# A mask write on VectorE for one score block in eight, with the value wave moved between two scores

## The reference

```
energy = einsum('nqhd,nkhd->nhqk', q, k)             # 16 heads of 32, 512 queries, 8192 keys
energy = where(mask == 0, -1e20, energy)
attention = softmax(energy / sqrt(512), axis=3)
out = einsum('nhql,nlhd->nqhd', attention, v) @ Wo.T + bo
x = x + out
```

## Time and profile before

| what | us |
|---|---|
| median of three runs | 4054.88 |
| the profiled execution, its own time | 4055.3 |
| its span, first to last instruction | 4053.6 |
| loop of the first attention in it, heads 0 to 14 up to the last maxima | 939.3 (417.85 to 1357.15) |
| a head of that loop, from one start to the next | 62.8 |

### The profile page before, as it was taken

The page is one execution under the profiler, slowest core; times in us unless marked ns, Lnnn a source line. Parts: engine busy times, 40 slices in busy tenths (PEclk is TensorE's granted clock), DMA queues, the critical chain, the costliest instruction groups (busy, mean ns, idle before and its releaser), DMA issues. The chain is left out here.

```text
span 4053.6 us, 51692 instructions
## 1 busy us (share of the span) xinstructions
PE 3772.0 (93%) x17986; PEld 2220.6 (55%) x17986; DVE 2806.8 (69%) x3519; ACT 2340.7 (58%) x3659; POOL 1873.0 (46%) x1133
## 2 busy tenths in 40 slices
PE   9999999999999976789999899999999988869998
PEld 7887444444444342247888644444444435448886
DVE  4334877777777368945888877777777644668888
ACT  2224677777777735423777626666666641537775
POOL 1001687787877718920000147888888830000001
PEclk9999999999999987889999979999999999979999
DMA  9997566666666512022888767777777640328887
GB/s 355 327 339 247 136 155 153 159 152 156 152 156 152 127 60 83 0 97 85 323 317 322 285 176 173 172 168 174 176 175 172 133 113 32 84 90 323 322 320 264
DMA packets 298957, 750.50 MB, mean 185 GB/s; under 512 B 56878, under 2 KB 90414, under 8 KB 264906
## 3 DMA queue, kind: packets, MB, share of 16 engines
q1 hardware_dynamic: 249306, 569.44, 41.7%
q0 software_dynamic: 49392, 177.76, 21.9%
HBM read 475.44 MB, written 98.96 MB: 142 GB/s over the span
## 5 line engine op out<-in xcount | busy, mean ns | idle before, releaser
L1026 ACT ACTIVATE prob<-psum 128x512 f32<-128x512 f32 x1628 | 918.0, 598 | 402.4 <-PE psum L902 373.1
L1222 POOL TENSOR_TENSOR den_pool<-den_pool,prob 128x1024 f32<-128x1024 f32 x405 | 1018.7, 2515 | 87.4 <-DVE den_pool L1127 33.2
L902 PE MATMUL psum<-q_stack,k_ring 98*128 98x512 f32 x2048 | 961.3, 500 | 20.5 <-ACT prob L1026 16.8
L1098 DVE CUSTOM_DVE_ANT_0 psum<-psum,mask_q 128x1024 f32<-128x1024 f32 x512 | 627.0, 1234 | 229.2 <-PE psum L864 213.4
L1094 DVE TENSOR_REDUCE row_max<-psum 128x1 f32<-128x1024 f32 x512 | 609.9, 1219 | 225.1 <-PE psum L864 219.5
L902 PEld LDWEIGHTS psum<-q_stack,k_ring 98*128 98x128 f32 x2048 | 395.7, 194 | 526.0 <-ACT psum L1032 199.2
L864 PE MATMUL psum<-k_ring,q_stack 96*128 96x512 f32 x2048 | 670.2, 409 | 12.0 <-DMA q_stack<-prob 5.2
L1982 DVE TENSOR_TENSOR weight_lo<-weight_raw,weight_hi 128x2048 fp32r<-128x2048 f32 x180 | 411.1, 2290 | 113.8 <-ACT weight_hi L1978 113.5
L913 PE MATMUL psum<-prob,x 128*32 128x512 f32 x3256 | 474.7, 608 | 3.2 <-ACT prob L1026 0.8
L864 PEld LDWEIGHTS psum<-k_ring,q_stack 96*128 96x128 f32 x2048 | 389.7, 194 | 97.8 <-issue 18.0
L2157 POOL DMA_DIRECT2D y_slots<-xnT x28 | 15.3, 548 | 860.0 <-ACT xnT L2261 860.0
(11 more groups left out here) (468 smaller groups left out, 6582.7 us busy)
## 6 DMA issues: line engine op xcount, KB each, us to landing
den_dma<-prob POOLq DMA_DIRECT2D x211, 512.0 KB, 5.1
k_ring<-k_hi SPq DMA_DIRECT2D x1024, 64.0 KB, 2.3
weight_raw<-in_L_ffn_Wu SPq DMA_DIRECT2D x60, 1024.0 KB, 7.3
weight_raw<-in_L_ffn_Wd SPq DMA_DIRECT2D x60, 1024.0 KB, 5.5
weight_raw<-in_L_ffn_w SPq DMA_DIRECT2D x60, 1024.0 KB, 6.6
den_dma<-xnT POOLq DMA_DIRECT2D x72, 512.0 KB, 5.0
k_ring<-k_lo SPq DMA_DIRECT2D x512, 64.0 KB, 2.6
w_o<-in_L_ffn_w SPq DMA_DIRECT2D x30, 1024.0 KB, 7.3
```

Source lines behind the costliest of these rows:

```text
L902: e.matmul(out, k_ring[:, n % kring, kt * P:(kt + 1) * P], q_stack[h % n_q][:], start=not masked, stop=True, skip_group_check=masked and b ...
L1026: e.activation(prob[b // 2 % n_p][:, b % 2, :], bank_of("block", b), ACT.Exp, scale=scale).then_inc(s_exp, 1)
L1098: e.tensor_tensor_reduce(out=max_banks(q), in0=max_banks(q), in1=masks[0][:, i, 2 * c2 * KC:2 * (c2 + 1) * KC], scale=1.0, scalar=-3.0e38, ...
L1222: e.tensor_tensor(den[:], den[:], tile, ALU.add).then_inc(s_dpool, 1)
```

## The change

Every block with b % 8 == 1, the second block of each step with g % 4 == 0, gets its mask from VectorE instead of from TensorE. VectorE's `mask_first` waits until the bank is free, writes `mask_k` times 2^67 into it with one `tensor_scalar`, and raises `s_predve`. It stands in VectorE's queue ahead of the reduction of the same step. On TensorE the mask matmul of that block is gone, its score waits for `s_predve` and adds to what lies in the bank, and in those steps the wave comes ahead of score 2g+1 instead of behind it. The sixteen heads have 128 such blocks.

```
+    def act_masks(b):
+        return masked and b % 4 == 2
+    def dve_masks(b):
+        return masked and b % 8 == 1
...  scores(b), TensorE
-                if masked and b % 4 == 2:
+                mask_is_there = act_masks(b) or dve_masks(b)
+                if act_masks(b):
                     e.wait_ge(s_pre, b // 4 + 1)
+                elif dve_masks(b):
+                    e.wait_ge(s_predve, b // 8 + 1)
                 else:
                     wait_for_bank(e, "block", b)
-                if masked and b % 4 != 2:
+                if masked and not mask_is_there:
                     e.matmul(out, k.ident_big[:], masks[1][:, t, :], start=True, stop=False)
                 e.matmul(out, k_ring[:, n % kring, kt * P:(kt + 1) * P], q_stack[h % n_q][:],
-                         start=not masked, stop=True, skip_group_check=masked and b % 4 == 2).then_inc(s_score, 1)
+                         start=not masked, stop=True, skip_group_check=mask_is_there).then_inc(s_score, 1)
...  the loop over steps, TensorE
+                if dve_masks(2 * g + 1):
+                    waves_after(h, p)
                 scores(2 * g + 1)
                 for q in second:
                     maxima(q)
-                waves_after(h, p)
+                if not dve_masks(2 * g + 1):
+                    waves_after(h, p)
...  VectorE
+            def mask_first(b):
+                wait_for_bank(e, "block", b)
+                e.tensor_scalar(bank_of("block", b), masks[1][:, b % KT, :], BIG, None, ALU.mult).then_inc(s_predve, 1)
...  the loop over steps, VectorE
+                if dve_masks(2 * g + 1):
+                    mask_first(2 * g + 1)
                 for q in maxima_at(g):
                     if q < H * PAIRS:
                         maxima(q)
```

More of the change, by code:

```diff
@@ L749, in cross_attention @@
     s_score, s_exp, s_wave = k.sem("s_score"), k.sem("s_exp"), k.sem("s_wave")
-    s_pre = k.sem("s_mask_first")
+    s_pre, s_predve = k.sem("s_mask_first"), k.sem("s_mask_first_dve")
     s_ddve, s_dpool, s_dsum = k.sem("s_den_dve"), k.sem("s_den_pool"), k.sem("s_den_sum")
```

## The result

The changed kernel takes 4064.43 us, the median of 18 runs (4059.87 to 4073.66), against 4056.56 for the kernel before (18 runs). The ratio of the two is 1.0022, 95% interval 1.0015 to 1.0028: slower by two parts in a thousand, within the bound of 0.3% that the prediction set for "no change". The profiled execution has a span of 4058.7, 5.1 more than before.

A forecast was written before the change was run, and what follows sets the result against it. The loop was taken to run at TensorE's pace. Fifteen heads +5.2, three heads more +1.2, head 0 +0.8 and head 15 +0.8 summed to +8.0 us on 4055.3, so 4063; range 4048 to 4080.

The forecast's parts named there:

- The ordinary step: Masked step away from VectorE's adds: the wave covers VectorE's mask, and TensorE saves one matmul, 0.22 us.
- The mask's length: VectorE's mask instruction: 0.69 us, taken from the 128x512 copy with one operand in PSUM.
- Steps 4 and 8: Where VectorE's adds put it behind: TensorE waits for late masks, 1.17 us in step 8; a head 1.47 late at step 9.
- Step 28: Late in each head, where `top_of_rows` holds VectorE: the mask is seen after TensorE wants it, 0.2 us lost.
- heads 4, 8 and 12: Heads with reciprocals: VectorE another 0.3 us behind in step 28 and 0.1 in step 24; +1.2 us for the three.
- step 24: In the three heads with reciprocals: these put VectorE 0.1 us behind there.
- Head 0: Its step 0 has no wave and saves nothing (+0.2); the mask meets a full VectorE chain at loop start, +0.8 us.
- Head 15: No maxima before the wave, which moves ahead by only 0.15 to 0.2; 0.1 us lost a step, +0.8 in all.
- what fifteen heads have in common: Per head +1.47 from steps 4 and 8, -1.32 from six other steps, +0.20 from step 28: +0.35, in all +5.2 us.
- cover everywhere: Rival: masks of steps 4 and 8 come in time, 119 or so save 0.22 each, -26 us, 4029; chance 0.10 with unseen gains.

The follow-up runs named there:

- e1: Changed kernel, with the masks of steps 4 and 8 of each head back on TensorE and the wave behind the scores there; ratio 0.9976 to the kernel before.
- e2: Kernel before with the wave moved as in the changed kernel, but every mask of VectorE left out and written by TensorE; ratio 0.9978 to the kernel before.
- e6: Changed kernel, with VectorE's adds of steps 4, 5 and 6 cut to 4 columns of 1024; ratio 0.9965 to the kernel before.
- e5: Changed kernel, with step 4's mask queued ahead of the add of step 3 and step 8's ahead of the reduction of step 7; ratio 1.0013 to before.
- e7: Changed kernel, with every mask of VectorE written twice, one after the other; ratio 1.0222 to the kernel before.
- e9_without_2: Kernel e8 without the moved wave in step 2; ratio 0.9967 to the kernel before.
- e4: Changed kernel, with VectorE's masks in most even steps but 4, 6, 8 and 30, 167 masks instead of 128; ratio 0.9965 to the kernel before.
- e8: Changed kernel, VectorE's masks only in steps 0, 12, 16, 20, 24, 28 (some heads excepted), wave also moved in 2, 4, 10, 14, 22, 26; ratio 0.9960 to before.
- e10: Kernel before with no mask on VectorE and the wave between the two scores in eleven steps of heads 0 to 14; ratio 0.9973 to the kernel before.
- e3: Changed kernel, all masks still on VectorE, but the wave left behind the second score; ratio 1.0326 to the kernel before.

## Why the prediction was right

The forecast was 4063 and 4064.43 was measured; +8.0 by the sum, +7.8 in the loop. By its steps:

- **The ordinary step**: 0.22 saved a step, as predicted, in the trace and in e1. Its reason was half wrong. I took it for the place of the removed matmul; e2 shows that 0.10 to 0.11 of it comes with the order alone, without VectorE. The times of the single instructions in the working are right; what they were summed up as, "one matmul, and no more", is not.
- **The mask's length**: 0.69 from the copy out of PSUM, 0.71 measured. The rule of the Trainium skill ("VectorE: DVE Perf Modes", "Why PSUM operands drop a tier") held here: no row near the 0.48 of the form in SBUF alone, the shortest of the 128 took 0.67.
- **Steps 4 and 8**: predicted 3.05 and 3.65, measured 3.06 and 3.67. For step 8 e6 shows that the adds of steps 4 to 6 are the cause and e5 that the mask's place is not; for step 4 e5 shows that its place behind the add of step 3 is. e7 shows that a longer mask counts twice on the way.
- **Step 28**: predicted 0.2 lost and 0.5 in heads 4, 8 and 12; measured nothing in the plain heads (2.32) and 0.42 in those three. Their step 24, predicted 0.1, lost nothing. The `tensor_scalar` starts right behind the small reductions, earlier than the reduction of the maxima did in the earlier trace rows.
- **Head 0**: predicted +1.15 with what it has in common with the others, measured +1.9. TensorE stood still 0.87 us for the first mask (step 0 +0.90) and then ran 3.4 us at half clock (step 1 +0.81). That the mask's wait brought the half clock is not shown: e9_without_2 has no mask of VectorE there, and its clock fell at 415.9 us, before the loop, for 10.2 us.
- **Head 15**: predicted +0.8, measured 0.0 (55.16 us to the last score in both), by luck. Steps 0, 4, 8 and 12 lost 0.2 each with the step behind, twice the 0.1 of the prediction. But in the kernel before, the clock was at half for 6.8 us from step 19 on, and in the changed one it was not (first row before, second after); its steps 20 and 21 took 2.74 us instead of 5.23, and later steps, 24 and 27 above all, gave the gain back.

```profile
1389.40:1396.20 6.80, 6.04 (x17) 1.90 (x17) 0.69 (x1) 3.96 (x8) 6.66 (x4) 0.50 0.59 115
```
```profile
1389.40:1396.20 6.80, 6.16 (x34) 1.82 (x34) 0.69 (x1) 5.00 (x11) 6.66 (x6) 1.00 0.40 77
```
- **Head 14**: it lost 0.78 instead of 0.35, which the prediction did not have either. Its last four steps have no maxima, and step 28, which a mask lengthens from 1.96 to 2.30 there, costs 0.34 instead of saving 0.12.
- **Two heads more**: 7 and 12 lost 0.65 and 0.44 in step 4, which no step of the prediction had. VectorE's add of step 3 lasted 1.87 us in head 7 instead of 1.22; GpSimd's adds of 2.6 us, the row below it, ended at 868.72, 0.8 after VectorE's began.

```profile
867.93 1.87 DVE L1140 TENSOR_TENSOR den_pool<-prob 128x1024 f32<-128x1024 f32 x1
```
```profile
863.51 5.21 POOL L1240 TENSOR_TENSOR den_pool<-den_pool,xnT 128x1024 f32<-128x1024 f32 x2
```

By terms, the 8.0 was 5.2 for what fifteen heads have in common, 1.2 for heads 4, 8 and 12, 0.8 for head 0 and 0.8 for head 15. Measured were 3.1, 1.4, 1.7 and 0.0, and another 1.6 in heads 7, 12 and 14 that stood in no term. The mechanism is right; that its sum came within 0.2 us of the measured 7.8 is luck, since the misses have both signs. The fastest rival, cover everywhere, failed where it was said to fail: in a chain without a gap.

## What to carry to other kernels

An engine that idles a quarter of a loop can still be full in the six steps where its extra work lies: before you give it a task in every n-th step, follow its queue through those steps, and leave these out. When a change has two parts, run each alone; here the reordering that was meant as cover is worth as much as the work that it covers. And when a loop gets shorter, look at the engine that just kept up. Here that was GpSimd: in e4, e8 and e10, the kernels with the most moved waves, a VectorE add came to begin under one of its adds in some heads and lasted longer, and in e4 ScalarE waited for its DMAs as well.

## What was not expected

- TensorE's granted clock can fall to half after a single stall in a stream that was otherwise full: in e7 behind 1.81 us of waiting in 12 of 15 heads, in e3 behind 1.67 us in 13 of 15. It stayed there for some 3.4 us, in three heads of e7 for 6.8. In most heads that cost 1.3 to 1.7 us (3.2 in those three), about as much again as the stall. The same stall in the same step had no drop in the other heads, and nothing here says why. Behind the 1.08 us of step 8 in the changed kernel it never fell. The kernel before has no drop in this loop up to head 14.
- A VectorE add of two SBUF tiles that begins while GpSimd runs an add of its own, also in SBUF, lasts until 1.08 us after GpSimd's has ended. The twelve profiles have 45 that began more than 0.14 us before that end; all ended 1.08 or 1.09 after it and took 1.27 to 3.22 us. All others took at most 1.23. The reduction of the maxima, with one operand in PSUM, shows nothing of it: 350 began under a GpSimd add in the changed kernel, the longest of 1.23 us. The Trainium skill ("SBUF — State Buffer", "SBUF: two separate sides") tells of a port pair that the two share: a VectorE instruction with two SBUF inputs gets it only when a GpSimd instruction that reads SBUF and started first has ended. The rows agree, but no kernel here moved such an add on purpose.
